# A graph kernel on one Trainium2 core: own halves of two pools taken every 8 and 12 columns instead of every 4 and 8

## What is computed

```
def _pool_max(h, edge_src, edge_dst):
    pooled = jax.ops.segment_max(h[edge_src], edge_dst, num_segments=N)
    ...
h1 = jax.nn.relu(embeddings @ Wp1.T + bp1)
p1 = _pool_max(h1, edge_src, edge_dst)
x = jax.nn.relu(jnp.concatenate([embeddings, p1], axis=1) @ Wm1.T + bm1)
p2 = _pool_max(x, edge_src, edge_dst)
y2 = jax.nn.relu(jnp.concatenate([x, p2], axis=1) @ Wm2.T + bm2)
x = _layernorm(y2 + x, ln2_g, ln2_b)
p3 = _pool_max(x, edge_src, edge_dst)
y3 = jax.nn.relu(jnp.concatenate([x, p3], axis=1) @ Wm3.T + bm3)
x = _layernorm(y3 + x, ln3_g, ln3_b)
```

## Time and profile before

| | us |
|---|---|
| median of three executions | 4963.57 (4955.61 to 4965.45) |
| the profiled execution | 4973.72, its span 4972.0 |
| second pool: first gather to last gather | 639.98 to 1097.26 |
| third pool: first gather to last gather | 1164.95 to 1640.43 |

### The profile page before, as it was taken

The page is one execution under the profiler, slowest core; times in us unless marked ns, Lnnn a source line. Parts: engine busy times, 40 slices in busy tenths (PEclk is TensorE's granted clock), DMA queues, the critical chain, the costliest instruction groups (busy, mean ns, idle before and its releaser), DMA issues.

```text
span 4972.0 us, 70678 instructions
## 1 busy us (share of the span) xinstructions
PE 3481.2 (70%) x18022; PEld 2634.2 (53%) x18022; DVE 2845.9 (57%) x8726; ACT 2119.5 (43%) x4948; POOL 3199.0 (64%) x3257
## 2 busy tenths in 40 slices
PE   3122189979999688788888888887889987962100
PEld 2011178867788565556655565555778873431000
DVE  6754334436444688787888878787544442124433
ACT  1000068955788343335333353333479974420000
POOL 4777677766767377774777747776057772027776
PEclk7555599989999899999999999999999998985555
DMA  5556566665656433333333333333166662246665
GB/s 181 192 171 215 193 201 221 222 206 186 203 197 228 147 104 104 104 105 97 103 105 105 104 92 104 104 105 106 64 205 214 213 213 75 102 150 207 206 204 190
DMA packets 275492, 776.56 MB, mean 156 GB/s; under 512 B 63777, under 2 KB 99874, under 8 KB 270882
## 3 DMA queue, kind: packets, MB, share of 16 engines
q0 software_dynamic: 155568, 425.01, 29.9%
q1 hardware_dynamic: 119538, 347.03, 18.2%
HBM read 454.85 MB, written 316.93 MB: 155 GB/s over the span
## 4 chain that ended last, share of the span: by engine, by line
PE 34%; DMA 9%; POOL 9%; issue 6%; DVE 5%; ACT 2%; DVEq 1%; SPq 0%; POOLq 0%; ACTq 0%
PE PS L1157 9%; PE PS L1363 8%; POOL HC L539 5%; PE PS L1355 5%; PE PS L1289 3%; DMA X<-table,idx_src 3%; PE PS L1050 3%; DMA HC<-table_typ,run_typ 3%; DMA HC<-table,idx_src 2%; POOL HC L515 2%; POOL X L515 1%; DVE work L1985 1%; PE PS L1344 1%; PE PS L1452 1%; PE PS L1044 1%
## 5 line engine op out<-in xcount | busy, mean ns | idle before, releaser
L1798 DVE SCALAR_TENSOR_TENSOR HC<-HC,run_rst 128x256 f32<-128x256 f32 x1858 | 901.9, 485 | 930.3 <-DMA HC<-table,run_max 288.3
L539 POOL DMA_INDIRECT HC<-table,run_max x1101 | 1088.7, 989 | 462.2 <-issue 288.1
L515 POOL DMA_INDIRECT HC<-table,idx_src x648 | 639.1, 986 | 352.6 <-DMA table<-B 156.0
L1157 PE MATMUL PS<-AM,ring 128*128 128x256 f32 x3600 | 794.9, 384 | 26.7 <-ACT ring L738 21.9
L1157 PEld LDWEIGHTS PS<-AM,ring 128*128 128x128 f32 x3600 | 692.8, 193 | 129.0 <-DVE HC L1798 23.3
L515 POOL DMA_INDIRECT X<-table,idx_src x600 | 602.9, 1005 | 182.9 <-issue 128.0
L1355 PE MATMUL PS<-AM,work 128*128 x3744 | 648.8, 285 | 20.5 <-DVE score L1985 19.1
L2041 DVE SCALAR_TENSOR_TENSOR HC<-HC,fcol,PS 128x257 f32 x1248 | 586.0, 470 | 102.6 <-PE PS L1363 91.2
L539 POOL DMA_INDIRECT HC<-table_typ,run_typ x391 | 379.0, 969 | 396.2 <-DMA table_typ<-HC 277.3
L539 POOL DMA_INDIRECT HC<-table_rel,run_rel x371 | 360.6, 972 | 283.0 <-DMA table_rel<-B 170.2
L1355 PEld LDWEIGHTS PS<-AM,work 128*128 128x128 bf16 x3744 | 373.9, 101 | 224.2 <-issue 72.6
(11 more groups left out here) (270 smaller groups left out, 5640.2 us busy)
## 6 DMA issues: line engine op xcount, KB each, us to landing
prefix<-HC SPq DMA_DIRECT2D x485, 512.0 KB, 3.4
table_typ<-HC SPq DMA_DIRECT2D x18, 1024.0 KB, 3.8
HC<-table,run_max POOLq DMA_INDIRECT x1101, 3.3
HC<-table,idx_src POOLq DMA_INDIRECT x648, 2.8
X<-table,idx_src POOLq DMA_INDIRECT x600, 2.8
HC<-table_typ,run_typ POOLq DMA_INDIRECT x391, 2.9
table_typ<-AM SPq DMA_DIRECT2D x6, 1024.0 KB, 3.8
HC<-table_rel,run_rel POOLq DMA_INDIRECT x371, 3.3
```

Of the source, the lines that this page charges most:

```text
L515: pool.indirect_dma_start(held(t)[:, 0:D], None, table, bass.IndirectOffsetOnAxis(ap=idx_src[:, t:t + 1], axis=0)).then_inc(landed[t % AHE ...
L539: pool.indirect_dma_start(run_slot(k), None, src, bass.IndirectOffsetOnAxis(ap=run_idx[s[1]][:, j:j + 1], axis=0)).then_inc(landed[k], 16)
L1157: last = nc.tensor.matmul(PS[:, (2, 5)[c % 2], h * D:(h + 1) * D], duos(s)[:, x % 4, b % 2, h * P:(h + 1) * P], rows, start=(b + h == 0), ...
L1798: V.scalar_tensor_tensor(run_slot(k), run_slot((j - 1) % SLOTS), run_rst[:, j:j + 1], fresh, fade, join).then_inc(pooled, 1)
```

## The change

Two edits that belong together. One more `yield` per block in `inside()` moves block b's own half on VectorE behind column 3+8b in the second pool and 3+12b in the third. `picks_first` gets the same step, so that TensorE and ScalarE place pairs and blocks by the new columns. The work of every engine is the same, instruction by instruction; its order is another.

```
         def picks_first(s, i):
 
-            return sum(1 for pair in pairs_in(s) if 4 * (s[2] - 1) * (i - 1) + 3 > pair[0] - 12)
+            return sum(1 for pair in pairs_in(s) if 4 * s[2] * (i - 1) + 3 > pair[0] - 12)
...
                                 if s[2] == 3:
                                     add_row(b, 3)
                                     yield
+                                if s[2] > 1:
+                                    yield
```

## The result

The changed kernel takes 4983.87 us (median; 4979.87 to 5000.89) against 4963.57 us before. The ratio is 1.0053, with a 95% interval of 1.0041 to 1.0065: slower by 0.53%, some 20 to 26 us. One of the five executions of the kernel before was a slow one, 5224.1 us, and the ratio leaves it out. The profiled execution took 5000.89 us, its span 4999.1 us, 27.1 us above that of before. The two pools themselves, from the first gather to the end of the last, grew by 25.5 us (15.4 and 10.1). Outside them two differences nearly cancel: the second pool began 8.8 us earlier than in the profile before, and the stages behind the third took 3341.5 us instead of 3331.5. In the nine other profiles on chips that run the kernel near 4970 us those stages took 3326 to 3337 us, so differences of this size come without the change.

A forecast was written before the change was run, and what follows sets the result against it. GpSimd's gathers bound the pools, plus stalls when TensorE is late beyond GpSimd's lead. The terms, +15.4 us (second pool) and +12.8 (third), sum to +28.2, a median of 4991.8 us, range 4968 to 5006.

The forecast's parts named there:

- Place and mechanism: GpSimd stalls, largest at gathers 184 to 200 (second pool) and 180 to 276 (third), because TensorE has more restarts.
- restarts: On TensorE, pairs that follow a block: 1.91 us idle before each, then 22.9 us mean for the pair, 24.8 together.
- "faster" rival: Duos ready ahead of the block make a restart cost 3.2 us less; all 30.3 us of stalls go, 4933; chance 0.06.
- Second pool, +15.4 forecast: Second pool's restarts between blocks go from three to eight; stalls 21.2 us against 5.8, +15.4 us.
- Third pool, +12.8 forecast: Third pool's restarts go from eight to thirteen; worst at block 21, late by 37.3 us against 24.5, +12.8 us.
- The sum: Both pools together +28.2 us: span 4972.0 to 5000.2, median 4963.6 to 4991.8 us.
- The clock: TensorE's lower clock slows five of eight restarted pairs, mean 22.9 us; 21.9 throughout would give +8, 23.51 throughout +40.

The follow-up runs named there:

- the duos ahead: Changed kernel, with ScalarE making the next pair's first two duos before it copies the blocks between pairs: 4937.84 us; the same in the kernel before: 4937.04 us.
- the run with 0: Changed kernel with the `picks_first` threshold at 0 columns instead of 12: 4971.97 us, ratio 1.0017 to the kernel before.

## Why the prediction was right

**Place and mechanism** held. In the changed kernel eight restarts of the second pool and thirteen of the third have 1.8 to 3.8 us of idle time before them, and with the duos ahead both that and all but 4.9 us of the stalls are gone. The "faster" rival named this very condition, duos that are ready ahead, and gave 4933; the runs that create it took 4937 and 4938. So the condition was right, and the change did not bring it.

**Second pool, +15.4 forecast, +15.4 measured** (472.7 less 457.3). The first pair started 5.2 us behind the first gather (636.33; 6.6 in the sum), took 24.13 us instead of 23.00, and the second pair started 36.4 us behind the first gather where 35.7 was worked out. Five of eight restarted pairs were slow, as in the rows that the mean came from. The second pair's own wait was larger than taken (3.79 us, behind a load for which ScalarE waited 1.9 us), and the first pair's start earlier; they cancel in part. That the sum was hit to the tenth is luck: the stalls grew by 17.4 us (23.2 less 5.8), and GpSimd's gathers themselves took 2.0 us less (449.5 instead of 451.5). The two pairs in the changed kernel's timeline:

```profile
636.33 24.13 PE L1157 MATMUL PS<-AM,ring 128*128 128x256 f32 x100 [4.20 <-ACT ring L738]
...
667.51 23.54 PE L1157 MATMUL PS<-AM,ring 128*128 128x256 f32 x100 [3.79 <-ACT ring L738]
695.12 23.51 PE L1157 MATMUL PS<-AM,ring 128*128 128x256 f32 x100 [1.90 <-ACT ring L738]
```

**Third pool, +12.8 forecast, +10.1 measured.** Block 21 was the worst, as worked out. From first pair to its product 337.5 us passed (1183.09 to 1520.59) against 342.9: five of the twelve restarted pairs were slow, mean 22.5 us instead of 22.9 (12 x 0.4 = 4.8), and the first pair was 0.8 shorter. The first pair, which I had left where it was, started 11.0 us behind the first gather instead of 8.6, since its load landed late (ScalarE waited 6.7 us for it). Together these take 3.0 us off the lateness that was worked out. Of the 10.1 us, 8.5 are stalls, and 1.6 a longer row of GpSimd's own gathers, 1.275 us each instead of 1.270.

```profile
1180.72 1.71 ACT L725 ACTIVATE work<-far_src,node_id 128x256 f32<-128x256 int32 x4 [6.72 <-DMA far_src<-picks]
...
1183.09 23.83 PE L1157 MATMUL PS<-AM,ring 128*128 128x256 f32 x100 [8.64 <-ACT ring L738]
```

**The sum.** +28.2 forecast; the two pools +25.5, the whole profiled execution +27.1, the medians +20.3. I had told the median as before's plus the sum, 4991.8; the measured 4983.87 is 7.9 us below. 2.7 us of that is the third pool's term; for the rest, 4991.8 lies inside the scatter of the executions (4979.87 to 5000.89).

**The clock.** The five of eight held for the second pool, six of thirteen were slow in the third. The rule of the Trainium skill's page "TensorE: Matmul & The Clock Gate", section "A second HAM failure mode: psum-queue depth-cycling", that short idle moments let the clock swing, is borne out in kind: with the idle time filled by four or six products, or gone, no restarted pair behind a pool's second is slow. Taken for every restart it would have been too much: 1.90 us of idle time stood before slow and fast pairs alike.

**What was not weighed.** Part of the stall is the 12-column threshold, which puts VectorE's wait ahead of the pair's own column; the run with 0 gives back 16 us of 25, up to 3.4 of them by fewer slow pairs. The kernel before has the same threshold and was not run without it, so how much of the change's own cost this is stays open. The sum had this inside it (it counted from the own half's column), but the text took all of it as restarts.

## What to carry to other kernels

Before work on a saturated engine is spread out, count how often its kind changes. Here each change from one producer's work to another's cost the start of that producer's chain, unless its first pieces were made ahead. Two duos made ahead were worth twice what the order of blocks had cost. And the stalls of a gather queue add up to the lateness of one place, the worst, beyond the queue's lead: sum the busy engine's work up to each place that others wait for, against the unstalled time of the gather that needs it.

## What the runs showed of the hardware

Filling 1.9 us of TensorE's idle time with products nobody reads brought 10.5 and 11.6 us per pool (four products in 1.89 us, at nine and fourteen places), and about 14 us in the time: the granted clock after them was 1.00 and the pairs took 21.85 us instead of up to 23.51. The loads of `far_src` landed 2.9 to 8.1 us after their issue in the changed kernel's profile, 2.9 to 5.4 before. And the same program took 30% longer on one chip than on the others (6457.55 us), with idle time on ScalarE that nothing in its trace explains.
